# A fused decoder on one core: the weighting product of the first cross-attention, put behind the turned maxima of the next pair

## The reference, cut to what matters

```python
q = x @ Wq.T + bq                       # 16 x 112 x 256, 16 heads of 16
k = context @ Wk.T + bk                 # 16 x 375 x 256
v = context @ Wv.T + bv
attn = einsum('bihd,bjhd->bhij', q, k) * SCALE
attn = softmax(attn, axis=-1)
out = einsum('bhij,bjhd->bihd', attn, v)
return out @ Wo.T + bo                  # then x = layernorm(x + this)
```

## Time and profile before

| | |
|---|---|
| median of 3 runs | 2634.37 us |
| the runs | 2634.37, 2632.79, 2640.01 us |
| the profiled execution | 2639.79 us, its span 2638.0 us, mean granted clock 0.863 |
| TensorE matmul | busy 2207.2 us, 84% of the span |
| TensorE weight load | busy 1522.6 us, 58% |
| VectorE | busy 1544.7 us, 59% |
| ScalarE | busy 708.9 us, 27% |
| GpSimd | busy 772.3 us, 29% |

### The profile page before, as it was taken

One profiled execution on the slowest core, in us unless ns is written; L12 is line 12 of the kernel. 1 busy time (PEld: TensorE's weight loads), 2 busy tenths in 40 slices (PEclk: granted clock), 3 DMA queues, 4 the chain that ended last, 5 costly groups with the idle time before them and its releaser, 6 DMA issues.

```text
span 2638.0 us, 37622 instructions
## 1 busy us (share of the span) xinstructions
PE 2207.2 (84%) x15316; PEld 1522.6 (58%) x15316; DVE 1544.7 (59%) x3090; ACT 708.9 (27%) x1355; POOL 772.3 (29%) x707
## 2 busy tenths in 40 slices
PE   7988899999799987999999999886677676777675
PEld 2333356667666656887887887775454542444432
DVE  7998844445233324555555655564699996445245
ACT  5544333333111122222222222221222221111132
POOL 3334458675200023443443443331100003011000
PEclk8777789888689998999999999998656757888887
DMA  4212362211100010001001001000601101400000
GB/s 140 86 55 79 99 143 57 55 52 50 40 13 1 0 76 1 1 1 63 1 1 63 1 1 47 1 1 0 146 27 36 29 21 25 99 0 0 1 0 28
DMA packets 63597, 101.68 MB, mean 39 GB/s; under 512 B 32361, under 2 KB 56930, under 8 KB 62210
## 3 DMA queue, kind: packets, MB, share of 16 engines
q1 hardware_dynamic: 63426, 99.28, 13.3%
HBM read 78.77 MB, written 20.50 MB: 38 GB/s over the span
## 4 chain that ended last, share of the span: by engine, by line
PE 68%; DVE 21%; POOL 3%; ACT 3%; issue 3%; DMA 1%; SPq 0%; POOLq 0%; DVEq 0%
PE PS L1408 8%; PE PS L1424 7%; PE PS L1162 4%; DVE top L2162 4%; PE PS L1325 4%; PE PS L1141 3%; DVE w_s L2171 3%; PE PS L871 3%; PE PS L858 3%; PE PS L2048 2%; DVE ln_st L265 2%; PE PS L2038 2%; PE PS L891 2%; PE PS L1353 2%; PE PS L1973 2%
## 5 line engine op out<-in xcount | busy, mean ns | idle before, releaser
L284 POOL TENSOR_SCALAR ln_ve<-ln_mv 128x2 f32<-128x2 f32 (+1 forms) x91 | 20.4, 224 | 1412.9 <-DVE ln_mv L268 1412.9
L1600 DVE TENSOR_TENSOR p_x<-PS,cols 128x1024 f32<-128x1024 f32 x112 | 129.3, 1217 | 155.4 <-PE PS L1370 155.3
L1662 POOL TENSOR_TENSOR q_x<-q_f,cols 128x2048 f32<-128x2048 f32 x56 | 208.7, 3747 | 7.7 <-ACT q_f L1520 7.7
L1020 DVE TENSOR_REDUCE XD<-PS 112x2 f32<-112x750 f32 x128 | 120.2, 941 | 120.7 <-PE PS L858 120.5
L858 PE MATMUL PS<-enc_w,q_s 32*112 32x375 f32 x512 | 172.8, 558 | 4.0 <-DVE XD L1020 4.0
L988 ACT ACTIVATE e_t<-PS 125x672 f32<-125x672 f32 x128 | 93.6, 731 | 192.8 <-PE PS L871 192.8
L452 PE MATMUL PS<-bc_parts,ident 96*128 96x448 bf16 x256 | 106.6, 521 | 41.9 <-DVE st_h L686 26.5
L1228 DVE SCALAR_TENSOR_TENSOR XA<-PS,gate_w,XA 112x256 f32<-112x256 f32 x128 | 61.9, 484 | 133.7 <-PE PS L1162 133.7
L1932 PE MATMUL PS<-dg,e_p 112*125 112x112 f32 x384 | 81.4, 405 | 63.9 <-ACT dg L2116 63.9
L871 PE MATMUL PS<-q_s,enc_w 32*125 32x112 f32 x1536 | 128.6, 301 | 2.4 <-ACT e_t L988 2.4
L1490 ACT ACTIVATE wb<-PS,cols 128x256 f32<-128x256 f32 x224 | 91.0, 473 | 140.3 <-PE PS L1408 140.3
(11 more groups left out here) (352 smaller groups left out, 4795.4 us busy)
## 6 DMA issues: line engine op xcount, KB each, us to landing
v_all_scratch<-v_st SPq DMA_DIRECT2D x16, 750.0 KB
v_t<-v_all_scratch SPq DMA_DIRECT2D x16, 750.0 KB
t_ring<-k_scratch SPq DMA_DIRECT2D x8, 784.0 KB, 11.1
enc_w<-in_enc_w SPq DMA_DIRECT2D x2, 3072.0 KB, 11.0
wc<-in_enc_w SPq DMA_DIRECT2D x2, 3072.0 KB, 11.3
k_all_scratch<-k_st SPq DMA_DIRECT2D x16, 375.0 KB
enc_w<-k_all_scratch SPq DMA_DIRECT2D x64, 93.8 KB, 3.5
ctx_k<-in_ctx SPq DMA_DIRECT2D x16, 281.2 KB
```

Of the source, the lines that this page charges most:

```text
L1020: dve.tensor_reduce(nm_w[0:T, g % 4, 64 * half + 16:64 * half + 49:32], PS[0:T, 2 * half:2 * half + 2, 0:S2], AX.X, ALU.max, negate=True). ...
L1600: last = dve.tensor_tensor(p_x[:, m, :, :, :], ps[1][:, m * P:(m + 1) * P].rearrange("p (h i) -> p h i", i=16).unsqueeze(2) .to_broadcast( ...
L1662: last = pool.tensor_tensor(q_x[:, c, :, :].rearrange("p t (h i) -> p t h i", i=16), q_f[:, k % 2, c, :].rearrange("p (t i) -> p t i", i=1 ...
```

## The change

The weighting product of group g moves from the even slot 2g + 2, where it stood ahead of the sums, the spread sums and the projection, to the odd slot 2g + 3, behind the turned maxima. All other uses stand right behind the shifted scores. ScalarE's copy of bank 6 moves from the first to the second slot of a batch. No semaphore, buffer or instruction is added or taken away.

```diff
--- before.py
+++ after.py
@@ -955,13 +955,9 @@
                         for a in range(2):
                             shifted(n, a, j)
                 for kind, i in uses:
-                    if kind in ("q", "x1"):
-                        shared[kind](i)
-                if n % 2 == 0 and 0 <= n // 2 - 1 < PAIRS // 2:
-                    weigh(n // 2 - 1)
-                for kind, i in uses:
-                    if kind not in ("q", "x1"):
-                        shared[kind](i)
+                    shared[kind](i)
+                if n % 2 == 1 and 0 <= (n - 3) // 2 < PAIRS // 2:
+                    weigh((n - 3) // 2)
 
         def xat_act(act):
             act.wait_ge(scaled, 2)
@@ -992,7 +988,7 @@
                     elif kind == "x1":
                         act.wait_ge(xt_ready, NQ - 1 + i + 1)
                         act.copy(XF[:, i, TOK - QT:TOK], xat_bank("x1", i)[:, 0:QT]).then_inc(xf_ready, 1)
-                if n % 8 == 0 and 1 <= n // 8 <= B:
+                if n % 8 == 1 and 1 <= n // 8 <= B:
                     b = n // 8 - 1
                     act.wait_ge(av_done, 4 * (b + 1))
                     if b >= 1:
```

## The result

| | before | after |
|---|---|---|
| median of the runs | 2633.58 us (4 runs, 2628.63 to 2640.01) | 2586.33 us (4 runs, 2582.42 to 2588.93) |
| the profiled execution's span | 2638.0 us | 2580.6 us |
| first to last exponential of the stage | 359.53 to 699.33, 339.8 us | 356.28 to 652.21, 295.9 us |

The changed kernel takes 0.9823 of the time before (95% interval 0.9811 to 0.9836): 47 us less. The sum had 33, for 2601.4. The range 2586 to 2611 holds the result by 0.3 us, and that is luck: a second set of runs of the same kernel gave 2583.4 (first experiment). The likeliest case's own range, 2594 to 2607, doesn't hold it.

A forecast was written before the change was run, and what follows sets the result against it. TensorE and ScalarE take turns in half the slots, leaving a 0.8 us hole in odd ones. Step gains of 34.1 us, about 1 at half clock, less 2 at GpSimd: 33 off 2634.4, so 2601.4 us; range 2586 to 2611.

The forecast's parts named there:

- The sum: First cross-attention stage: all gains and losses together give 33 us less, 2601.4 us.
- The likeliest case: Whole kernel: the forecast as it stands, 2601.4 us, own range 2594 to 2607, chance 60%.
- The steps: Times between exponentials: odd slots stay 1.91 us; even ones fall to 2.57, 1.91, 1.91, 2.79; 34.1 us saved.
- The cover: Odd slots: the exponential demands 1.05 us between blocks anyway, so maxima plus moved product, 0.95, cost 0.
- GpSimd at the first norm: Stage's first norm would come 2.0 us before GpSimd finishes the convolution kernel: 2 us lost.
- The waits that move: Product, exponential buffers, copy of summed heads, value loads: all in time; copy early by 0.45 us, turned sums by 0.25.
- Rival C: Copy of the summed heads or another signal arrives late, holding the turned sums; nothing gained, 2634 us; 4%.
- over the seven such slots ... about 1 us more: Half-clock slots with sums: a pair gains 0.7 us against 0.56 and 0.45 counted, about 1 us more.
- Rival A: Stage's half-speed stretches, about 21 us, become fewer; if half go, 10 us more gained, 2591 us; 18%.
- Rival B: Odd slots: gaps between maxima, product and block make the step 2.0 us instead of 1.91; 2609 us; 14%.
- Rival D: Even slots lose their densest work, so the clock falls more; with 20 half-speed pairs 2651 us; 4%.
- the slack of the spread sums' slots: Even slots with spread sums: even if sums need 0.99 us instead of 0.88, 1.84 stays under 1.91.

The follow-up runs named there:

- first experiment: The changed kernel run again with no edit: 2583.4 us, ratio 0.981 against the kernel before.
- the norm was split: VectorE takes norm statistics at once and applies them one batch a slot later: ratio 0.9967 in the kernel before, 0.9759 (2571.5 us) in the changed one.
- the last experiment: Weighting product cut to a third in the changed kernel (2608.0 us) and the kernel before (2648.9 us), or made four thirds in the changed kernel (2587.6 us).
- the early root: Changed kernel with GpSimd's step of the first norm put ahead of the last three rounds of powers: ratio 0.9823 against the kernel before.

## Why the prediction was right, and where it was mis-sized

**The steps.** Odd slots at 1.91 with the product added, even ones at 2.57, 1.91, 1.91 and 2.79: found to 0.01 us. The cover is the exponential's round trip: the product costs nothing in it, whole or a third, and 0.11 us when it is a third longer. The sum of all steps at full clock, 34.1 in the prediction, reads 34.4. It left out two slots of the first batch, where input transposes stood with a product: 2.12 and 2.11 before, 1.91 now, 0.4 together.

**GpSimd at the first norm.** Foretold as 2 us. VectorE stood 2.2 us longer, and the step behind the norm is 10.36 us against 7.91 behind the second norm, where GpSimd is in time: 2.5 us. The two norms also differ in the clock of the queries behind them, so the wait is the better measure. Right, and low by the 0.4 us of the first batch at most. What I didn't have is that curing it brings something else: about 1 us is given back where VectorE's applications run beside GpSimd.

**The waits that move.** The copy was to run from about 1.1 to 1.65 after the end of the block; with the block's end at 375.27 it runs 1.08 to 1.61 behind it (376.35 to 376.88). The turned sums follow at 377.18 and the next exponential at 377.37, 1.9 and 2.1 behind it as foretold, and ScalarE kept its beat. Rival C had no ground.

**The term that was mis-sized** is "over the seven such slots ... about 1 us more": I kept the half-speed stretches of the old order where they stood, and priced the change inside them. The price was right (odd slots 3.2 and even ones 3.15 foretold, 3.23, 3.19 and 3.13 in the fourteenth batch), but of some 22 us that the low clock cost in the stage 12 went. Rival A named it, with 10 us of 21 and 18%. The argument against it, that the stretches follow the norms and the narrow sums, which stay, was half right: the stretch behind the third norm stayed, as the changed kernel's TensorE shows (the wait for VectorE in brackets, and the first matmul behind it at 0.93 where it takes 0.56 at full clock),

```profile
589.94 0.49 PE L871 MATMUL PS<-q_s,enc_w 32*125 32x112 f32 x5
593.88 0.93 PE L858 MATMUL PS<-enc_w,q_s 32*112 32x375 f32 x1 [3.46 <-DVE XD L1016]
```

and went when the norm was split. That of the last batch stayed too, shorter. The two that started at residual transposes went with the change, and with the products of the sum slots alone. That it is the filled hole behind them is the likely reading, but not shown: with just these six products moved, half-speed slots stayed in both batches, and with the norm split they came back in the seventh batch of the changed kernel. Why the clock falls in one slot and not in another like it stays open.

**Rival B** did not come in as time: maxima, product and block follow each other in 0.25 and 0.71, as they did apart, and the order of the first two makes no difference. But its mechanism is there. Behind the product the next work starts 0.71 us later where it uses the array in another way and 0.60 where it uses it alike; with a third of the product these are 0.32 (turned sums) and 0.22 (spread sums); and with four thirds, in the changed kernel,

```profile
382.66 0.97 PE L891 MATMUL PS<-e_t,v_t 125*32 125x112 f32 x32
383.57 0.56 PE L858 MATMUL PS<-enc_w,q_s 32*112 32x375 f32 x1
```

0.91. So a block of keys costs 0.20, and about 0.11 of the 0.71 comes once, with the change of use (the spread sums are the only work behind a product that uses the array alike, so something else about them isn't ruled out). The Trainium skill, TensorEngine Tiling (Array Packing), "Key Properties", says that changing the tiling mode drains the engine; the trace agrees with something of that kind, at 0.11 us. The 0.71 held it already, and the slack of the spread sums' slots hid the one that was added, as the prediction had it.

**Rival D**, the clock falling for want of dense work, was wrong for the change as a whole, and variants show that such losses exist: with only the products of the sum slots moved new half-speed slots took 12 us, and with a third of the product 36 us in the kernel before (steps worth 21 less, time 15 more). The rule that I cited in rival A (the Trainium skill, TensorE: Matmul & The Clock Gate, "What's actually happening"), that the throttled state is the default and activity releases it, agrees: over the two kernels and the three variants of the last experiment the granted clock of the stage, 0.77 to 0.98, rises with the matmul records per us. This is a weak sign, since a low clock also stretches the time.

## What to carry to other kernels

Where two engines take turns, read the start times of the one that paces them: the longer of a round trip and of the work between two beats gave the four steps of the changed kernel to 0.01 us, and tells which work to move under which beat. Then ask what the change does to the clock: with the hole of every second slot filled, a third more came than the steps say, and leaving work out made the kernel slower. Which slots gain or lose by it could not be told ahead here. A step that stands behind other work in a queue (here a norm's root behind the whole kernel build on GpSimd) becomes late as soon as the rest gets faster; price it by its slack.

## What was not expected of the hardware

- **Less work, more time.** Two thirds of the product left out cost the kernel before 15 us and the changed one 22 to 25 us, in slots at the low clock (granted clock 0.90 to 0.77 and 0.93 to 0.83 over the stage), while the steps at full clock were shorter or the same.
- **The clock repeats.** Two profiles of the kernel before, and two of the changed one, have half-speed slots in the same places, and stage lengths that agree to 0.1 us. Two variants of the kernel before that began 5 us earlier, with a first step of 4.82 us, have others in batches whose order is the same; the changed kernel with the early root began so too and kept its own.
- **VectorE beside GpSimd.** Four norm applications of 112 x 256 took 2.41 us beside GpSimd's two-input products of 0.46 to 0.50 us and 1.38 without; one of them takes 0.41 alone, and here the four lie between 0.54 and 0.95. The Trainium skill, SBUF — State Buffer, "SBUF: two separate sides", says that the two engines share a port pair which, where both need it, one of them holds for a whole instruction while the other waits. A later stage of the same run agrees, beside a longer instruction of GpSimd:

```profile
2143.11 2.34 POOL L2280 TENSOR_TENSOR x<-x,enc_w 112x1024 f32<-112x1024 f32 x1
2143.17 3.40 DVE L277 TENSOR_SCALAR x<-XA,ln_mv,ln_rs 112x256 f32<-112x256 f32 x4 [2.18 <-POOL ln_rs L285]
```

  Of these four the first takes 2.43 us: it ends 0.15 behind GpSimd's instruction.
- **Still open.** Behind the stage, from its last exponential to the end of the span, the kernels of this study take 1928.4 to 1942.0 us: 1938.7 and 1935.3 for the two profiles of the kernel before, 1928.4 for both of the changed one. No instruction differs there, and other kernels lie on either side (1938.4 and 1942.0 in variants of the kernel before, 1934.3 and 1941.1 in variants of the changed one). The two profiled executions differ by 57 us: 3 ahead of the stage, 44 in it and 10 behind it, where the medians differ by 47. So the 3 us of the median's gain that the stage doesn't explain, or more, may be the phase in which the later stages meet the clock. No run separates it.
